# Heads' outputs reordered through DRAM, and score and row products dealt out singly on TensorE

## The reference

```python
# x, ctx: [16, 128, 512]; 8 heads of 16 rows each; tokens run along the last axis
s = SCALE * log(k_length)                      # one scale a batch
attn = softmax(s * einsum('bhdq,bhdk->bhqk', qh, kh), axis=-1)
out  = einsum('bhqk,bhdk->bhdq', attn, vh)     # reshaped to [16, 128, 512]
x = x + out                                    # x1
x = x + moe(layernorm(x))                      # gate, top 2 of 8, silu(x w1) * (x w3) w2
```

## Time and profile before

| | |
|---|---|
| median of 3 runs | 1180.6 us (1180.52 to 1184.16) |
| the profiled execution, its own time | 1181.91 us |
| its span, first to last instruction | 1180.4 us |
| mean granted TensorE clock in it | 0.957 |
| busy share of the span | PE 88%, DVE 58%, POOL 55%, ACT 36% |

### The profile page before, as it was taken

How to read it: one execution, slowest core, us unless ns; L and a number is a source line. 1 busy time by engine, 2 the same in 40 slices (tenths; PEclk the granted TensorE clock), 3 DMA queues, 4 the chain that set the end, 5 groups by cost and what they waited for, 6 DMA issues and landing times.

```text
span 1180.4 us, 20555 instructions
## 1 busy us (share of the span) xinstructions
PE 1039.7 (88%) x5098; PEld 415.4 (35%) x5099; DVE 685.0 (58%) x1029; ACT 426.6 (36%) x751; POOL 653.9 (55%) x618
## 2 busy tenths in 40 slices
PE   1899998989898999871799999999999999999980
PEld 0223333323232333220344444444444444444430
DVE  5867777767776777414354546535464455543356
ACT  8267776767676777751111111111101111111110
POOL 5454777676767675223287806618384383810475
PEclk9799999999999999995899999999999999999995
DMA  6575656666656554002797755737676475843778
GB/s 192 166 217 151 189 177 175 180 180 181 180 167 185 151 169 135 30 31 68 201 229 183 208 161 146 222 89 216 175 189 193 98 206 152 227 89 81 167 191 283
DMA packets 212715, 195.70 MB, mean 166 GB/s; under 512 B 137376, under 2 KB 176288, under 8 KB 207264
## 3 DMA queue, kind: packets, MB, share of 16 engines
q1 hardware_dynamic: 197760, 122.26, 40.4%
q0 software_dynamic: 14336, 71.87, 18.7%
q10 hardware_dynamic: 576, 1.05, 0.3%
HBM read 111.48 MB, written 53.00 MB: 139 GB/s over the span
## 4 chain that ended last, share of the span: by engine, by line
PE 66%; DMA 11%; issue 7%; POOL 6%; DVE 6%; ACT 2%; POOLq 1%; SPq 1%; DVEq 0%
PE rows L1175 30%; PE heads_out L1175 14%; PE heads_out L1089 6%; PE scores L1076 6%; PE rows L1062 5%; DMA rb<-recips_dram 4%; DMA W<-parts_dram 4%; DVE nm L773 3%; PE misc L1139 2%; ACT W L655 1%; POOL us L525 1%; POOL us L528 1%; POOLq L595 1%; PE misc L1131 1%; POOL W L598 1%
## 5 line engine op out<-in xcount | busy, mean ns | idle before, releaser
L1175 PE MATMUL rows<-W,U 128*128 (+1 forms) x1776 | 391.5, 381 | 17.3 <-DMA U<-stage 17.0
L773 DVE TENSOR_REDUCE nm<-rows 128x2 f32<-128x1024 f32 x256 | 304.9, 1219 | 98.8 <-PE rows L1062 91.6
L655 ACT ACTIVATE W<-scores 128x512 f32<-128x512 f32 x512 | 283.5, 596 | 148.0 <-PE scores L1076 146.7
L1175 PEld LDWEIGHTS rows<-W,U 128*128 128x128 bf16 x1776 | 174.2, 98 | 228.6 <-issue 21.4
L720 ACT ACTIVATE U<-rows 128x512 f32<-128x512 f32 x78 | 46.3, 597 | 509.8 <-PE rows L1175 497.9
L1175 PE MATMUL heads_out<-W,U 128*128 x888 | 199.4, 381 | 2.3 <-DMA U<-U 2.1
L1062 PE MATMUL rows<-W,U 96*128 96x512 bf16 x512 | 148.1, 399 | 56.1 <-DMA W<-parts_dram 28.2
L980 DVE TENSOR_TENSOR U<-rows,U 128x512 bf16<-128x512 f32 x78 | 53.9, 691 | 229.2 <-ACT U L720 229.0
L1076 PE MATMUL scores<-U,W 128*128 128x512 bf16 x512 | 170.7, 390 | 5.8 <-ACT W L655 5.1
L437 POOL TENSOR_TENSOR W<-U,W 128x2048 bf16<-128x2048 f32 x42 | 171.6, 4085 | 7.7 <-POOL W L436 7.7
L436 POOL TENSOR_SCALAR W<-U 128x2048 bf16<-128x2048 f32 x42 | 80.8, 1923 | 147.6 <-PE rows L1175 139.3
(11 more groups left out here) (170 smaller groups left out, 718.9 us busy)
## 6 DMA issues: line engine op xcount, KB each, us to landing
U<-wpack_dram POOLq DMA_DIRECT2D x42, 1024.0 KB, 5.9
parts_dram<-U SPq DMA_DIRECT2D x32, 384.0 KB, 4.1
U<-parts_dram SPq DMA_DIRECT2D x32, 384.0 KB, 4.0
W<-parts_dram SPq DMA_DIRECT2D x32, 384.0 KB, 5.1
stage<-slots_dram SPq DMA_DIRECT2D x39, 257.0 KB, 3.0
expert_out_dram<-U SPq DMA_DIRECT2D x39, 256.0 KB, 3.1
parts_dram<-U SPq DMA_DIRECT2D x32, 256.0 KB, 4.0
stage<-wpack_dram POOLq DMA_DIRECT2D x12, 512.0 KB, 6.3
```

Of the source, the lines that this page charges most:

```text
L655: s.activation(probs[:, w % 2, j, kk, :], sc[u % 2][:, :], ACT.Exp) \
L773: v.tensor_reduce(nm[:, bb.parity, 2 * k:2 * k + 2], p1[k % 2][:, :].rearrange("p (c k) -> p c k", c=2), AX_X, ALU.max, negate=True).then_ ...
L1175: ins = m.matmul(bank, part_of(s_part, k), W[:, bass.ds(at_w, 512)], start=(k == 0 and n == 0), stop=(k == n_chunks - 1 and n == 2))
```

## The change

1. The selector product, its matrix `selu` and ACT's copy to `us` go. SP stores both halves of `og` whole (256 KB each, `store_heads`) in place of the rows of sums; `den` and `us` are loaded from that.
2. In TensorE's order score and row products are dealt out singly: score, rows, score, values, score, rows, score. Before, two row units stood together between the groups of four scores.
3. On POOL two one-column steps go (`-mean` for the prepared batch and for z): the mean is subtracted directly.
4. On DVE the reciprocals stand after the reduction of unit 6 in place of after unit 5, the statistics `st1` stand ahead of unit 6, and the statistics of x1 stand one reduction later (after unit 14).

```diff
-ENGINE_STEPS = {"prep": 10, "keys": 4, "z": 4, "route_a": 3, "route_b": 3}
+ENGINE_STEPS = {"prep": 9, "keys": 4, "z": 3, "route_a": 3, "route_b": 3}
...
+            def store_heads(b, g):
+                sp.dma_start(heads_dram[bass.ds(b.n, 1), g].rearrange("o p q -> (o p) q"), og[:, g, :]) \
+                    .then_inc(heads_out[g], 16)
...
                     sp.wait_ge(S["og_ready"], b.n * 2)
+                    store_heads(pv, 1)
+                    heads = heads_dram[bass.ds(pv.n, 1)].rearrange("o g (j r) q -> (o g j) r q", r=32)
                     for g in range(2):
-                        sp.dma_start(sums_dram[bass.ds(pv.n, 1), 4 * g:4 * g + 4].rearrange("o h q -> (o h) q"),
-                                     og[16:113:32, g, :]).then_inc(S["sums_out"], 16)
-                    sp.wait_ge(S["sums_out"], b.n * 32)
-                    sp.dma_start(den[:, :], sums_dram[bass.ds(pv.n, 1)].rearrange("o h (p f) -> (o h p) f", f=32)) \
+                        sp.wait_ge(heads_out[g], b.n * 16)
+                        sp.nop().then_inc(S["sp_held"], 1)
+                    sp.dma_start(den[:, :], heads[:, DH, :].rearrange("h (p f) -> h p f", f=32)) \
                         .then_inc(S["den_in"], 16)
+                    if b.within(2, B):
+                        sp.wait_ge(S["z_ready"], b.n - 1)
+                        sp.nop().then_inc(S["sp_held"], 1)
+                        sp.wait_ge(S["x1_kept"], b.n - 1)
+                        sp.nop().then_inc(S["sp_held"], 1)
+                    sp.dma_start(us[:, :], heads[:, 0:DH, :]).then_inc(S["us_in"], 16)
...
+                if b.within(0, B - 1):
+                    sp.wait_ge(S["og_ready"], b.n * 2 + 1)
+                    sp.nop().then_inc(S["sp_held"], 1)
+                    store_heads(b, 0)
...
-                    st.step(g.tensor_scalar(psc[:, 3:4], mean, -1.0, 0.0, ALU.mult, ALU.add))
...
                     st.step(g.tensor_tensor(norm[:, :], xres[:, bass.ds(pbt.n, 1), :].rearrange("p o q -> p (o q)"),
-                                            psc[:, 3:4].to_broadcast([P, L]), ALU.add))
+                                            mean.to_broadcast([P, L]), ALU.subtract))
...
-                    st.step(g.tensor_scalar(zsc[:, 2:3], mv2[:, 0:1], -1.0, 0.0, ALU.mult, ALU.add))
-                    st.step(g.tensor_scalar(z[:, pv.parity, 0:D], us[:, :], zsc[:, 2:3], zsc[:, 1:2], ALU.add, ALU.mult))
+                    st.step(g.tensor_scalar(z[:, pv.parity, 0:D], us[:, :], mv2[:, 0:1], zsc[:, 1:2], ALU.subtract, ALU.mult))
...
-                        if u % 4 == 0:
-                            rows_unit(4 * w + u // 2)
                         if full:
                             score(w, u)
+                        if u % 4 == 0:
+                            rows_unit(4 * w + 2 * (u // 4))
+                        if u in (1, 5):
+                            kk = u // 4
+                            if w == 0 and behind:
+                                values(pv, 3, kk)
+                            if w > 0 and full:
+                                values(b, w - 1, kk)
+                        if u % 4 == 2:
+                            rows_unit(4 * w + 2 * (u // 4) + 1)
...
-                        if (w, u) == (1, 2) and behind:
...
-                            for gr in range(2):
-                                ins = m.matmul(misc[:, :], selu[:, gr, :], og[:, gr, :], start=(gr == 0),
-                                               stop=(gr == 1))
-                            ins.then_inc(S["u_ready"], 1)
...
-                        if u % 4 == 3:
-                            rows_unit(4 * w + u // 2)
```

More of the change, by code:

```diff
@@ L207, in build @@
         st_in = [[sem(f"stack{i}{j}") for j in range(2)] for i in range(2)]
+        heads_out = [sem(f"heads_out{i}") for i in range(2)]
         slots_out = [sem(f"slots_out{i}") for i in range(2)]
@@ L681, in slot @@
                 exps(1, range(0, 4))
-                if pv.within(0, B - 1):
-                    act.wait_ge(S["u_ready"], b.n)
-                    if pv.within(1, B - 1):
-                        act.wait_ge(S["z_ready"], b.n - 1)
-                        s.nop().then_inc(S["act_held"], 1)
-                        act.wait_ge(S["x1_kept"], b.n - 1)
-                    s.activation(us[:, :], misc[:, :], ACT.Copy).then_inc(S["us_ready"], 1)
                 exps(1, range(4, 8))
@@ L803, in slot @@
                 maxima(range(4, 6))
-                if pv.within(0, B - 1):
-                    dve.wait_ge(S["den_in"], b.n * 16)
-                    if pv.within(1, B - 1):
-                        dve.wait_ge(S["rec_out"], b.n * 16 - 16)
-                    v.reciprocal(rden[:, :], den[:, :]).then_inc(S["rec_ready"], 1)
                 lb = b.plus(3)
@@ L820, in slot @@
                     v.bn_aggr(mv1[:, lb.parity, :], st1[:, :]).then_inc(S["st1_ready"], 1)
-                maxima(range(6, 8))
+                maxima(range(6, 7))
+                if pv.within(0, B - 1):
+                    dve.wait_ge(S["den_in"], b.n * 16)
+                    if pv.within(1, B - 1):
+                        dve.wait_ge(S["rec_out"], b.n * 16 - 16)
+                    v.reciprocal(rden[:, :], den[:, :]).then_inc(S["rec_ready"], 1)
+                maxima(range(7, 8))
                 if routes:
@@ L856, in slot @@
                     pt = parts[:, 0]
[L857 removed]
+                    q_steps.step(v.tensor_scalar(us[:, :], xres[:, 0, :], mv1[:, 0, 0:1], psc[:, 2:3], ALU.subtract, ALU.mult))
                     q_steps.step(v.tensor_copy(pt[:, 0, :], us[:, :]))
@@ L876, in slot @@
                         .then_inc(S["m_ready"], 1)
-                maxima(range(12, 13))
-                maxima(range(13, 14))
+                maxima(range(12, 15))
                 if pv.within(0, B - 1):
@@ L889, in slot @@
                     v.bn_aggr(mv2[:, :], st2[:, :]).then_inc(S["st2_ready"], 1)
-                maxima(range(14, 15))
                 maxima(range(15, 16))
@@ L1119, in slot @@
                             reader = (S["gate_used"], b.n - 1)
-                        if u in (1, 5):
-                            kk = u // 4
-                            if w == 0 and behind:
-                                values(pv, 3, kk)
-                            if w > 0 and full:
-                                values(b, w - 1, kk)
                         if (w, u) == (0, 7) and ahead:
@@ L1133, in slot @@
                             reader = (S["vt_ready"], b.n + 2)
-                        if (w, u) == (1, 2) and behind:
+                        if (w, u) == (1, 6) and pv2.within(0, B - 1):
                             if reader:
                                 pe.wait_ge(*reader)
-                            pe.wait_ge(S["og_ready"], b.n * 2)
-                            for gr in range(2):
-                                ins = m.matmul(misc[:, :], selu[:, gr, :], og[:, gr, :], start=(gr == 0),
-                                               stop=(gr == 1))
-                            ins.then_inc(S["u_ready"], 1)
-                            reader = (S["us_ready"], b.n)
-                        if (w, u) == (1, 6) and pv2.within(0, B - 1):
-                            pe.wait_ge(*reader)
                             pe.wait_ge(S["mask_ready"], b.n - 1)
```

28 lines of the change are left out of this document (11 added, 17 removed).

## The result

The changed kernel takes 1225.6 us (median of 4 runs, 1219.34 to 1227.14) against 1181.9: slower by a ratio of 1.0358, interval 1.0316 to 1.0400. The forecast was 1166.5 us and the range ended at 1178. The profiled execution took 1227.14 us, with a span of 1225.6 and a mean granted clock of 0.938.

The account below looks back on a forecast made before the run. POOL's program was taken to bound the attention loop. Gains of 7.0 + 2.6 + 1.7 + 0.5 + 1.8 + 1.0 = 14.6 us off 1181.9 gave 1167.3, or 1166.0 against the median; forecast 1166.5 us, range 1155 to 1178.

Parts of the forecast that it names:

- The two full-width steps that now read the mean keep their width and their number of operands, so I leave them at their price.: On POOL: dropping two one-column steps saves 0.46 and 0.41 us, together 0.87 us a batch; the full-width steps cost the same.
- TensorE then waits some 2 us at unit 12, on an engine with slack.: On TensorE at row unit 12: the wait for the reload of the parts grows from 0.98 to some 2 us.
- The reload comes when it came.: On SP's queue: the parts' stores start 0.6 to 0.9 us later, but the reload of the parts keeps its time.
- the transfers' rival: Rival: the transfers' chain takes over, rb up to 2.1 us later each batch, no net change, 1178 to 1182; chance 0.17.
- the ring: Not forecast; named after measuring: z write, query half, parts' stores, reload, unit 12, reductions, statistics, z; 34.07 us in the slot shown.
- The statistics of x1, one reduction later, cost nothing where POOL is late.: On DVE: there DVE waits for POOL anyway; elsewhere a reduction of some 1.2 us stands before them, within the range.
- The later reciprocals come in the shadow of the stores of the parts: On DVE: the reciprocals' later place falls during the parts' stores, before the reload; no cost was entered in the sum.
- POOL's program as the bound of the old loop.: In the attention loop POOL's chain of short steps sets the 30.58 us period; two steps less give 7.0 us over 8 periods.
- The new order: On TensorE: 0.16 us dearer per four scores, 1.3 us a batch; slack in the loop; 1.8 us gained over batches 11 to 13.
- The slower one: Rival: TensorE's idle time brings the low clock into every slot, 3.4 us lost a slot, some 8 us, 1189; chance 0.08.
- TensorE's own 27.75 us: TensorE's need for a slot with row units where POOL does not hold it: 28.15 - 1.7 + 1.3 = 27.75 us.
- 0.60 + 0.12 + a quarter of 0.17: Chance of faster by over 0.3%: POOL's beat shortened 0.60, TensorE as the bound 0.12, a quarter of transfers take over 0.17.

Follow-up runs that it names:

- only_z_step: The kernel before with only z written in one step that subtracts the mean: 1191.5 us, ratio 1.0082.
- fill_the_wait: The changed kernel with 14 unread products of 512 columns put on TensorE ahead of unit 12 in every slot: 1206.3 us, ratio 1.0216.
- stats_earlier: The changed kernel with the statistics of x1 on VectorE moved from behind the maxima of unit 14 to behind those of unit 12: 1208.6 us, ratio 1.0210.
- only_transfers: The kernel before with only the heads' transfers through DRAM in place of the selector product: 1215.3 us, ratio 1.0283.
- only_dve_places: The kernel before with only the later places on VectorE for the reciprocal and the statistics of x1: 1198.4 us, ratio 1.0127.
- us_behind_parts: The changed kernel with x1's statistics behind unit 12's maxima, and the load of us moved behind the parts' stores on SP's queue: 1190.2 us, ratio 1.0060.
- undo_order: The changed kernel with the old order of score and row products on TensorE put back: 1235.2 us, ratio 1.0436.

## Why the prediction was wrong

1. **"The two full-width steps that now read the mean keep their width and their number of operands, so I leave them at their price."** For the query half's step right: 1.04 us before and after. For z wrong: 0.76 became 2.07 us, 0.9 us a batch lost where 0.41 was to be gained. The width and the number of operands were weighed, the operation was not. only_z_step measured +9.9 us, not -6.6 (0.41 in 16 batches).
2. **"TensorE then waits some 2 us at unit 12, on an engine with slack."** The wait was foreseen and came at 3.9 us. That it costs nothing is the step that failed first of all: behind unit 12 stand the transposed maxima and the reductions of VectorE, behind these the statistics of x1, and behind these POOL. An engine's slack is not that of those who wait for it. And the wait brought the low clock, which lengthened just that piece; fill_the_wait gave 19 of the 44 us back, stats_earlier, which only takes the statistics out from behind the late reductions, 17.
3. **"The reload comes when it came."** It did not. Counted from z it was issued 2.0 us later in the changed kernel and 1.4 later in only_transfers (means of the eight loop periods). The stores of the parts left SP as foreseen, 0.6 us later, but their landing, put at the 2.8 us of the earlier trace rows, took 4.1 to 5.0 us behind the load of us (the last of the three). The 2.8 are a median over the stores of both halves; those ahead of the reload took 2.3 to 2.6 us before. The slot on which the prediction rested, with the reload at 271.87 and the wait of 0.98 us, was one of the three late ones. Nor was it the 16th score that freed the reload before. In the eleven slots from batch 0 to 10 it left 0.95 or 0.96 us behind the reciprocals' store each time, while its distance from the parts' stores went from 3.1 to 4.8 us; and when only_dve_places delayed that store, the reload came later with it. With this falls what the prediction held against the transfers' rival, that the reload and not the reciprocals stood ahead of rb. The later reload also held back rb; the place of the load of us is worth 18 us for both once the ring through VectorE is open (us_behind_parts).
4. **"The statistics of x1, one reduction later, cost nothing where POOL is late."** Wrong in a kernel otherwise unchanged: the two places together cost 1.27%. POOL is late only until it has written x1; then DVE must have its reduction behind it, and with the new place it is still in it for half a microsecond in the slot shown and starts the statistics 2.07 us after x1 in the mean of the loop. The longest wait of POOL for the mean rose from 3.6 to 5.0 us. "The later reciprocals come in the shadow of the stores of the parts" failed too, since the reload stands behind their store in the queue; how the loss divides between the two stays open.
5. **POOL's program as the bound of the old loop.** This held in the main: 0.46 us less in the query half gave 7.8 us, and only_z_step, 0.90 us a batch dearer on POOL, cost 9.9 of the 14.4 us that 16 batches make. Neither is one for one, so the bound is not POOL's program alone. The changed kernel has another bound, the ring.
6. **The new order** was priced as slack in the loop and 1.8 us behind it. It gained 3.3 alone and 9.6 in the changed kernel. In undo_order den is issued 10.18 us after z in place of 9.07 (means of the loop), so the old order brings the heads' output later in the slot and what follows with it; that this is all of its price is not shown.
7. **The rivals.** The slower one, low clock in every slot, named one of the causes, with a chance of 0.08 and a price of 8 us. The price was too low because it added the loss to TensorE's own 27.75 us and not to the ring, and it left out the z step and the places. The Trainium skill ("TensorE: Matmul & The Clock Gate", "Why this matters for your kernels") warns of idle gaps between bursts; the trace agrees in each of the six slots between 176 and 398 us.
8. **A small slip in the chances.** 0.60 + 0.12 + a quarter of 0.17 is 0.76, not 0.77.

## What to carry to other kernels

When work was taken here from an engine that then waited for a transfer, it only waited longer. Before calling that free, follow what stands behind the waiting instruction, engine by engine, until the chain comes back to itself or ends; if it comes back, each delay in it can be paid in every period. Look at what a wait is in every period and not in one, since the slot that shows it may be the exception. Price an instruction by its operation and form, not by its shape: a step saved by another operation may cost more than the step.

## What the runs showed of the hardware

- On POOL a tensor-scalar step of 128 x 512 f32 took 0.76 us as add and multiply with two scalars from tiles, and 2.07 us as subtract and multiply (2071 to 2086 ns in 16 of them), with the mean in either of two tiles. The tensor-tensor step of the same width took 1.04 us both as add and as subtract. The Trainium skill ("GPSIMD Engine Reference", section 3.1) gives 769 ns as the best case for 512 elements; the adding form agrees, the subtracting one took 2.7 times that.
- A wait of 3.9 us on TensorE was followed by the clock of 0.50 (in the slot shown from about 268 to 275 us, so for longer than the wait itself); waits of 0.62 and 0.98 us at the same place were not. The stretch at the low clock outlasted its cause and slowed the very units that were late.
- With a load of 256 KB ahead of three stores on one queue, the last of these landed 4.4 to 4.7 us after its issue (stats_earlier, slots of the loop); with the load behind them 2.3 us in most slots (us_behind_parts), as in the kernel before, which has no such load.
